# A two-layer cross-attention kernel on one core: TensorE's first loop holds one batch, its products become pairs, and one slot's order and one transpose move

## The chip, the cores and the metric

The kernel runs on one core of a Trainium2 chip. The metric is device microseconds of one execution. TensorE multiplies matrices into PSUM; VectorE (DVE), ScalarE (ACT) and GpSimd (POOL) do the elementwise work, and SyncE (SP) issues nearly all transfers. Each engine runs its own instruction stream in order and waits on counting semaphores.

## The reference

```python
x = x + _L0_xattn_ref(_layernorm(x), ctx_768, Wq, Wk, Wv, Wo, bo)     # 16 heads of 64, softmax over 77 keys
x = x + _L0_ffn_ref(_layernorm(x), w_gate, w_up, w_down)              # silu(gate) * up, hidden 768
x = x + _L1_xattn_ref(_layernorm(x), ctx_768, Wq, Wk, Wv, Wo, bo)
x = x + _L1_ffn_ref(_layernorm(x), rhs)                               # rounded to 8 bits, scaled back
```

x is 32 batches of 256 rows by 256 numbers (float32), the context 32 batches of 77 rows by 192. Layer 0 is the first two lines, layer 1 the last two.

## The kernel before

A first part (to about 210 us) computes the keys and values of both layers and prepares the weights. Every operand is split into a high and a low float16 part, so each product is three terms (high x high, high x low, low x high).

The main part walks through steps h = 0 to 65: steps 0 to 31 are the batches of layer 0, steps 32 to 63 those of layer 1. A step has four slots, u = 0 to 3, one for four heads each. Work on one batch is spread over several steps: in step h TensorE computes the scores of batch h, the queries of two slots ahead, the weighted values of three slots back, the output projection of batch h-1, and the feed-forward of batches h-2 and h-3. `lay[d]` is the layer of the batch at step h+d, or None. One step of layer 0 is called a batch below.

In the third slot (u = 2) of layer 0, TensorE's order is: scores of row tile 0, `down(0)` (the feed-forward's last product for rows 0 to 127; 12 products), the queries (12 products), scores of row tile 1, `down(1)` (12 products for rows 128 to 255), `gate_up(1)` (the feed-forward's first products for hidden columns 128 to 255; 8), `project` (12) and `weigh_values`. The names of the tiles: `kb` holds keys, `qT_h`, `qT_l` the queries' parts, `xT` the turned normalised rows that the queries are made from, `wdT` with `hT_h`, `hT_l` are the operands of `down`, `x2T` those of `gate_up`, `oT_h`, `oT_l` those of `project`, `pT` and `vb` those of `weigh_values`.

`product` writes a product either as one matmul of 128 columns of weights, or, with `halved`, as a pair of matmuls of 64 columns, each with its own half of PSUM's partitions. `weigh_values` is always pairs. In layer 0 the products of the third slot, `down` and `gate_up(1)` are whole, all others are pairs. (In the profile, L301 is a half of a pair, L299 a whole product, L1126 `down`.)

The results of `gate_up` and `down` go to two PSUM banks in turn. A program (`uses`, `released`) decides which: the order of uses in a step of layer 0 is gate_up(4), gate_up(5), gate_up(0), down(0), down(1), gate_up(1), gate_up(2), gate_up(3). A use waits until its bank's last use has been read. `down(1)` thus takes the bank of `gate_up(0)`, and waits on `s_hf`, which VectorE raises when `hidden(0)` (tile `hf`, L1320) has read that bank.

VectorE's order in the third slot: statistics of the next rows, `sigmoid_gate(0)`, `maxima` of row tile 0, `out_rows(0)` (reads `down(0)`'s bank, tile `y`, L1330), `shift` (`nmr`), the low part of `oT`, `hidden(0)` (`hf`), a reciprocal, `maxima` of row tile 1, the low part of the queries, `out_rows(1)`.

The turned rows `xT` have two buffers, used in turn by even and odd batches. SP issues the transposing transfer for batch h+2 in the last slot of step h (`turn_rows`), which waits on `s_q` until the buffer's last queries are made; the queries of batch h+1 in slot u = 2 wait on `s_xd` for theirs. SP also issues the transposes of the probabilities (`pT`), keys, values and rows, in one queue.

TensorE, ScalarE and VectorE run steps 4 to 27 and 36 to 59 as hardware loops whose body holds two steps (`bodies`, `LOOPS`); SP and GpSimd have all steps written out.

Of the kernel before, what the change touches and what calls it, by code (L numbers as in the profile page):

```python
# [40 lines left out]
P = 128  # L41
HEADS, DH = 16, 64
UNITS = 4
# [7 lines left out]
def xattn_ffn_kernel(nc, x, ctx, wq0, wk0, wv0, wo0, bo0, w_gate, w_up, w_down,  # L51
                     wq1, wk1, wv1, wo1, bo1, rhs, out):
    B, NQ, D = x.shape
# [27 lines left out]
    with stack:  # L81
# [184 lines left out]
        x_src = [x.rearrange("b (t p) d -> b p t d", p=P), mid_d.rearrange("b (t p) d -> b p t d", p=P)]  # L266
        def turned_rows(par, part):

            return xT[par][:, :, part, :, :]

# [9 lines left out]

        def turn_rows(sp, b):

            sp.wait_ge(s_x16l, b)
            after(sp, s_q, UNITS * (b - 1))
            sp.dma_start_transpose(xT[b % 2][:, :, :, :, :].rearrange("p t r k q -> p (t r k) q"),
                                   x16[:, :, :, :].rearrange("p t r d -> p (t r d)")).then_inc(s_xd, 16)
# [17 lines left out]
        def queries(pe, u, l, par, o, halved):  # L304
            for a in range(PPU):
                w = slice((u * PPU + a) * P, (u * PPU + a + 1) * P)
                oo = o[:, a, :].rearrange("p (t q) -> p t q", q=P)
                terms = [(ww, part, k) for k in range(KT) for ww, part in
                         ((wq_h[l], 0), (wq_h[l], 1), (wq_l[l], 0))]
                for q, (ww, part, k) in enumerate(terms):  # L310
                    last = product(pe, oo, ww[:, k, w], xT[par][:, :, part, k, :], halved, start=(q == 0),
                                   stop=(q == len(terms) - 1))
            last.then_inc(s_q, 1)
# [57 lines left out]
        with nc.Block() as block:  # L371
            @block.sync
            def _(sp):
# [57 lines left out]
                i = NG - 1  # L431
# [16 lines left out]
                load_rows(2)  # L448
                turn_rows(sp, 1)
                store_keys(i, 1, 1)  # L450
# [495 lines left out]
        for first, last in LOOPS:  # L946
            assert (last - first) % 2 == 0
            assert all(kinds[h] == kinds[first + (h - first) % 2] for h in range(first, last))

        def bodies(eng, body):  # L950

            done = 0
            for first, last in LOOPS:
                for h in range(done, first):
                    body(h, h, *kinds[h])
                with eng.Fori(first, last, 2) as h:
                    body(h, first, *kinds[first])
                    body(h + 1, first + 1, *kinds[first + 1])
                done = last
            for h in range(done, NB + 2):  # L960
                body(h, h, *kinds[h])

        with nc.Block() as block:

            @block.sync
            def _(sp):
# [33 lines left out]
                def body(h, like, lay, plan):  # L1000
# [13 lines left out]
                    for u in range(UNITS):  # L1014
# [14 lines left out]
                        if u == 0 and lay[-2] == 0:  # L1029
                            turn_second_rows(h - 2)  # L1030
                        if u == 1 and lay[0] is not None:
                            after(sp, s_pv, n - 2)
                            load_values(0, at_own, lay[0])
# [16 lines left out]
                        if u == 3 and lay[3] == 0:  # L1050
                            sp.wait_ge(s_xn, QT * (h + 3))
                            sp.dma_start(x_in[:, :, :], batch_of(x_src[0], b_first)).then_inc(s_x, 16)
                        if u == 3 and lay[2] == 0:
                            turn_rows(sp, h + 2)
                        if u == 2 and lay[-3] == 0:
# [11 lines left out]
            def _(pe):  # L1067
                def paired(u, lay):

                    return lay[0] == 1 or u != 2  # L1070

                def scores(k, u, t, k_need, halved):
# [13 lines left out]
                def project(k, u, l):  # L1086

                    pe.wait_ge(s_ol, k + 1)
                    for t in range(QT):
                        for a in range(PPU):  # L1090
                            ts, m = slice(t * P, (t + 1) * P), u * PPU + a
                            for q, (oo, ww) in enumerate(((oT_h[u % 2], wo_h[l]), (oT_l[u % 2], wo_h[l]),
                                                          (oT_h[u % 2], wo_l[l]))):
                                first = u == 0 and t == 0 and a == 0 and q == 0
                                last = product(pe, OA[:, t, :], oo[:, a, ts], ww[:, m, :], u != (1 if l == 1 else 2),
                                               start=first, stop=(u == UNITS - 1 and a == PPU - 1 and q == 2),
                                               skip_group_check=True)
                    if u == UNITS - 1:
                        last.then_inc(s_oa, 1)
# [14 lines left out]
                def gate_up(c, o):  # L1114
                    for a, w in ((0, wgT), (1, wuT)):
                        oo = o[:, a, :].rearrange("p (t q) -> p t q", q=P)
                        terms = [(k, part) for k in range(KT) for part in range(2)]
                        for q, (k, part) in enumerate(terms):
                            last = product(pe, oo, w[:, k, c * P:(c + 1) * P], x2T[:, :, part, k, :], c != 1,
                                           start=(q == 0), stop=(q == len(terms) - 1))  # L1120
                    last.then_inc(s_g, 1)

                def down(t, o):
                    terms = [(c, hh) for c in range(HC) for hh in (hT_h, hT_l)]
                    for q, (c, hh) in enumerate(terms):
                        last = pe.matmul(o[:, 0, :], hh[:, c, t * P:(t + 1) * P], wdT[:, c, :], start=(q == 0),  # L1126
                                         stop=(q == len(terms) - 1))
                    last.then_inc(s_d, 1)
# [8 lines left out]
                def body(h, like, lay, plan):  # L1137
                    n = UNITS * h

                    def bank(*use):  # L1140

                        where, before = plan[use]
                        if before is not None:
                            pe.wait_ge(*released(before[0], h + before[1]))
                        return RG[where]

                    for u in range(UNITS):
# [9 lines left out]
                        if u == 3 and lay[-2] == 0:  # L1157
                            gate_up(2, bank("gu", 2))
                        if ("q", u) in plan:
                            if u == 2 and lay[1] == 0:  # L1160
                                pe.wait_ge(s_xd, 16 * (h + 1))
                            if u == 2 and lay[1] == 1:
                                pe.wait_ge(s_xl, h + 3 - B)
                            queries(pe, (u + 2) % UNITS, lay[(u + 2) // UNITS], (like + (u + 2) // UNITS) % 2, bank("q", u), paired(u, lay))
                        if u == 2 and lay[-2] == 1:
# [29 lines left out]

                bodies(pe, body)


            @block.scalar
            def _(act):  # L1200
                def body(h, like, lay, plan):
# [27 lines left out]
                    for u in range(UNITS):  # L1229
# [28 lines left out]
                        if u == 1 and lay[1] == 1:  # L1258
                            act.wait_ge(s_xt, h + 3 - B)
                            high(act, turned_rows((like + 1) % 2, 0),  # L1260
                                 bank("turned_x", 0).rearrange("p k (t q) -> p t k q", q=P)).then_inc(s_xh, 1)
# [38 lines left out]
            def _(dve):  # L1300
                def body(h, like, lay, plan):
# [47 lines left out]
                    for u in range(UNITS):  # L1349
# [65 lines left out]
                        if u == 1 and lay[1] == 1:  # L1415
                            dve.wait_ge(s_xh, h + 3 - B)
                            low(dve, turned_rows((like + 1) % 2, 1),
                                bank("turned_x", 0).rearrange("p k (t q) -> p t k q", q=P),
                                turned_rows((like + 1) % 2, 0)).then_inc(s_xl, 1)
                        if u == 1 and lay[-1] == 1:  # L1420
# [131 lines left out]
```

## Time and profile before

| | |
|---|---|
| median of 3 runs | 1631.79 us (1630.43 to 1633.48) |
| the profiled execution | 1632.44 us, its span 1630.6 us |
| mean granted clock of TensorE | 0.994 of full speed |
| TensorE (PE) busy | 1568.4 us, 96% of the span |
| VectorE, ScalarE, GpSimd busy | 1358.4, 1379.6, 1270.9 us (83%, 85%, 78%) |
| TensorE's matmuls | 25178 |

A row of the timeline is one instruction, or several alike in a row: start in us from the span's beginning, time in us until the last of them ends, engine, line, operation, tiles, partitions by columns, count. Matmuls overlap: one takes 0.27 us from start to end, but the next starts 0.11 us after it, so what a product costs is the distance between starts. PE is the matmul, PEld the load of its weights, which runs ahead.

### The profile page before, as it was taken

The page shows a single profiled execution, that of the slowest core. Times are in us where ns is not written, and L with a number is a line of the kernel's source. Part 1 is how long each engine was busy: PE and PEld are TensorE (multiplying, and loading weights), DVE is VectorE, ACT ScalarE, POOL GpSimd, SP SyncE. Part 2 cuts the span into 40 slices and gives each one's busy share as a digit, 9 for nine tenths or more (in the row PEclk, how much of TensorE's full clock was granted, in tenths as well). Part 3 has the DMA queues.
Part 4 walks back from the last instruction along what each step waited for, and adds up shares of the span by engine and source line. Part 5 has one row for each costly group of instructions (what it writes and reads, how often), then busy time and mean ns, then how long its engine had stood idle before and what let it go on. Part 6 is the DMA issues. An engine that isn't in the chain of part 4 may idle for free.

```text
span 1630.6 us, 70351 instructions
## 1 busy us (share of the span) xinstructions
PE 1568.4 (96%) x25178; PEld 1420.3 (87%) x25178; DVE 1358.4 (83%) x3519; ACT 1379.6 (85%) x5665; POOL 1270.9 (78%) x1892
## 2 busy tenths in 40 slices
PE   7999978999999999999999999999999999999995
PEld 4655668999999999999999999989999999999994
DVE  5777767888888888888888887888899899989885
ACT  5665677889998998998898888888999999999993
POOL 3300058898998988988988988778999999999984
PEclk9999999999999999999999999999999999999998
DMA  8975679897787787787787988889899889989995
GB/s 239 324 281 226 223 183 170 169 176 174 172 175 178 165 179 176 166 180 172 166 181 171 176 168 160 151 173 193 190 200 199 190 190 200 199 189 190 197 182 107
DMA packets 732248, 305.79 MB, mean 188 GB/s; under 512 B 621424, under 2 KB 717584, under 8 KB 730064
## 3 DMA queue, kind: packets, MB, share of 16 engines
q1 hardware_dynamic: 730272, 297.29, 82.1%
q0 software_dynamic: 1840, 6.82, 1.3%
q8 instruction: 69, 1.13, 0.3%
q14 instruction: 67, 0.55, 0.1%
HBM read 87.72 MB, written 65.54 MB: 94 GB/s over the span
## 4 chain that ended last, share of the span: by engine, by line
PE 35%; POOL 30%; issue 12%; DVE 5%; DMA 3%; ACT 1%; POOLq 0%; SPq 0%; ACTq 0%; DVEq 0%
PE psum L301 24%; POOL pr L1481 10%; POOL p L1488 8%; POOL p L1484 6%; PE psum L1110 4%; PE psum L299 4%; POOL hT_l L1471 3%; POOL rs L361 2%; DMA pT<-p 2%; PE psum L1126 2%; PE psum L292 1%; DVE oT_l L330 1%; DVE x L1460 1%; POOL y L1509 1%; DMA x2T<-x 1%
## 5 line engine op out<-in xcount | busy, mean ns | idle before, releaser
L1225 ACT ACTIVATE ex<-psum,nmax 128x77 f32<-128x77 f32 x2048 | 638.0, 335 | 46.2 <-DVE nmax L1342 37.1
L1225 ACT ACTIVATION_READ_ACCUMULATOR ex<-psum,nmax 128x1 f32 x2048 | 443.1, 216 | 0.0
L1488 POOL TENSOR_TENSOR p<-pr,p 128x308 f16<-128x308 f32 x512 | 413.1, 807 | 38.4
L1481 POOL TENSOR_TENSOR pr<-ex,rden 128x308 f32<-128x308 f32 x512 | 369.1, 721 | 63.7 <-DVE rden L1347 63.1
L301 PE MATMUL psum<-xT,wq_h 128*64 128x256 f16 x3552 | 304.5, 273 | 0.0
L1342 DVE TENSOR_REDUCE nmax<-psum 128x4 f32<-128x308 f32 x512 | 241.2, 471 | 63.6 <-PE psum L301 53.7
L1484 POOL CAST p<-pr 128x308 f16<-128x308 f32 x512 | 241.7, 472 | 43.0 <-DMA pT<-p 10.7
L301 PE MATMUL psum<-xT,wq_l 128*64 128x256 f16 x1776 | 245.9, 273 | 0.0
L301 PE MATMUL psum<-kb,qT_h 128*64 128x154 f16 x3584 | 228.0, 231 | 11.1 <-DVE qT_l L333 6.9
L301 PE MATMUL psum<-wo_h,oT_h 128*64 128x256 f16 x1536 | 214.2, 275 | 12.2 <-DVE oT_l L330 11.2
L1110 PE MATMUL psum<-pT,vb 77*64 77x256 f16 x3072 | 213.0, 274 | 0.6 <-DMA pT<-p 0.6
L301 PE MATMUL psum<-wo_h,oT_l 128*64 128x256 f16 x1536 | 212.6, 273 | 0.0
L301 PE MATMUL psum<-wo_l,oT_h 128*64 128x256 f16 x1536 | 212.6, 273 | 0.0
L330 DVE TENSOR_TENSOR oT_l<-psum,oT_h 128x512 f16<-128x512 f32 x256 | 175.7, 686 | 24.8 <-ACT oT_h L316 24.1
L301 PE MATMUL psum<-kb,qT_l 128*64 128x154 f16 x1792 | 196.1, 230 | 0.0
L301 PEld LDWEIGHTS psum<-kb,qT_h 128*64 128x64 f16 x3584 | 179.8, 110 | 14.2 <-DVE qT_l L333 9.3
L301 PEld LDWEIGHTS psum<-xT,wq_h 128*64 128x64 f16 x3552 | 190.3, 110 | 0.8 <-issue 0.6
L316 ACT ACTIVATE oT_h<-psum 128x512 f16<-128x512 f32 x256 | 153.9, 601 | 26.1 <-PE psum L1110 19.5
L333 DVE SCALAR_TENSOR_TENSOR qT_l<-psum,qT_h 128x512 f16<-128x512 f32 x256 | 174.0, 680 | 0.0
L1110 PEld LDWEIGHTS psum<-pT,vb 77*64 77x64 f16 x3072 | 164.3, 110 | 11.0 <-issue 7.7
L316 ACT ACTIVATE qT_h<-psum 128x512 f16<-128x512 f32 x256 | 154.9, 605 | 1.0 <-PEq L371 1.0
L361 POOL TENSOR_TENSOR rs<-ve,half_neg 128x2 f32<-128x2 f32 x127 | 88.5, 696 | 56.4 <-DVE ve L346 52.9
(167 smaller groups left out, 3805.4 us busy)
## 6 DMA issues: line engine op xcount, KB each, us to landing
keys<-ks SPq DMA_DIRECT2D x16, 1232.0 KB, 5.3
kb<-keys SPq DMA_DIRECT2D x256, 77.0 KB, 2.6
vb<-vals SPq DMA_DIRECT2D x128, 154.0 KB
vals<-vs SPq DMA_DIRECT2D x64, 256.0 KB, 3.1
x_pair<-in_x_dram SPq DMA_DIRECT2D x32, 256.0 KB, 3.1
pT<-p SPq DMA_TRANSPOSE x512, 3.3
x_res<-in_x_dram SPq DMA_DIRECT2D x32, 256.0 KB, 3.0
mid_x<-y SPq DMA_DIRECT2D x32, 256.0 KB, 2.4
```

Source lines behind the costliest of these rows:

```text
L299: return pe.matmul(o, w, x, **flags)
L301: last = pe.matmul(o[b * DH:(b + 1) * DH], w[:, b * DH:(b + 1) * DH], x, **flags)
L316: return act.activation(dst, src, ACT.Copy, scale=scale)
L330: return dve.tensor_tensor(dst, src, hi, ALU.subtract)
L333: return dve.scalar_tensor_tensor(out=qT_l[i][:, :, :], in0=src, scalar=Q_DOWN, in1=qT_h[i][:, :, :], op0=ALU.mult, op1=ALU.subtract)
L361: pool.tensor_tensor(rs[:, :], ve[:, :], half_neg[:, :], ALU.pow).then_inc(s_inv[k], 1)
L1110: last = pe.matmul(OV[b * DH:(b + 1) * DH, a, :], vb[u // 2][:, part, c:c + DH], pT[u][0:NK, pp * HPU + hd, :], start=(q == 0), stop=(q == 2))
L1225: last = act.activation(ex[i][:, t, b, :], SC[:, t, b * NK:(b + 1) * NK], ACT.Exp, bias=nmax[i][:, t, b:b + 1], accum_out=den[i][:, t, b:b ...
L1342: dve.tensor_reduce(nmax[i][:, t, :], SC[:, t, :].rearrange("p (h k) -> p h k", k=NK), AX_X, ALU.max, negate=True).then_inc(s_m, 1)
L1481: pool.tensor_tensor(pr[:, t, :, :], ex[i][:, t, :, :], r, ALU.mult).then_inc(s_p, 1)
L1484: pool.tensor_copy(d[:, t, 0, :, 0:NK], pr[:, t, :, :]).then_inc(s_ph, 1)
L1488: pool.tensor_tensor(d[:, t, 1, :, 0:NK], pr[:, t, :, :], d[:, t, 0, :, 0:NK], ALU.subtract).then_inc(s_pl, 1)
```

## The change

- TensorE's loop over steps 4 to 27 has a body of one step (24 turns in place of 12). The other engines' loops, and TensorE's second loop, keep two steps.
- Every product of layer 0 in the loop, and `down` and `gate_up(1)`, is a pair of 64 columns.
- From batch 4 on, the turned rows have one buffer (`home`). Their transposing transfer is issued a step later than before, in SP's first slot behind the transpose of `x2T`, and waits on `s_q` until all queries of batch h (the last of them in TensorE's slot u = 1) are made.
- In the third slot of steps 3 to 33 (`late`), TensorE runs `down(1)` directly behind `down(0)`, and the queries behind the scores of row tile 1.

```diff
-        def turned_rows(par, part):
+        def home(b):
+            return 1 if b in (1, 3) else 0
+        def turned_rows(b, part):
-            return xT[par][:, :, part, :, :]
+            return xT[home(b)][:, :, part, :, :]
...
-        def turn_rows(sp, b):
+        def turn_rows(sp, b, like):
             sp.wait_ge(s_x16l, b)
-            after(sp, s_q, UNITS * (b - 1))
+            if like <= 4:
+                after(sp, s_q, UNITS * (like - 1))
+            else:
+                sp.wait_ge(s_q, UNITS * b)
...
-            for first, last in LOOPS:
+            for (first, last), step in zip(LOOPS, steps):
                 for h in range(done, first):
                     body(h, h, *kinds[h])
-                with eng.Fori(first, last, 2) as h:
-                    body(h, first, *kinds[first])
-                    body(h + 1, first + 1, *kinds[first + 1])
+                with eng.Fori(first, last, step) as h:
+                    for i in range(step):
+                        body(h + i if i else h, first, *kinds[first])
...
+                        if u == 0 and lay[1] == 0 and like >= 4:
+                            turn_rows(sp, h + 1, like + 1)
...
-                        if u == 3 and lay[2] == 0:
-                            turn_rows(sp, h + 2)
+                        if u == 3 and lay[2] == 0 and like <= 2:
+                            turn_rows(sp, h + 2, like + 2)
...
-                def paired(u, lay):
-                    return lay[0] == 1 or u != 2
...
-                                last = product(pe, OA[:, t, :], oo[:, a, ts], ww[:, m, :], u != (1 if l == 1 else 2),
+                                last = product(pe, OA[:, t, :], oo[:, a, ts], ww[:, m, :], l == 0 or u != 1,
...
-                            last = product(pe, oo, w[:, k, c * P:(c + 1) * P], x2T[:, :, part, k, :], c != 1,
+                            last = product(pe, oo, w[:, k, c * P:(c + 1) * P], x2T[:, :, part, k, :], True,
...
-                        last = pe.matmul(o[:, 0, :], hh[:, c, t * P:(t + 1) * P], wdT[:, c, :], start=(q == 0),
-                                         stop=(q == len(terms) - 1))
+                        last = product(pe, o[:, 0, :], hh[:, c, t * P:(t + 1) * P], wdT[:, c, :], True, start=(q == 0),
+                                       stop=(q == len(terms) - 1))
...
-                            scores(n + u, u, 0, 32 * (h + 1), paired(u, lay))
+                            scores(n + u, u, 0, 32 * (h + 1), True)
                         if u == 2 and lay[-3] == 0:
                             pe.wait_ge(s_hlp, len(LOW_POOL) * (h - 2))
                             pe.wait_ge(s_hld, len(LOW_DVE) * (h - 2))
                             down(0, bank("down", 0))
...
+                        late = u == 2 and lay[-3] == 0 and lay[-2] == 0
+                        if late:
+                            down(1, bank("down", 1))
+                        else:
+                            make_queries(u)
...
-                            scores(n + u, u, 1, 0, paired(u, lay))
+                            scores(n + u, u, 1, 0, True)
+                        if late:
+                            make_queries(u)
...
-                        if u == 2 and lay[-3] == 0:
+                        if u == 2 and lay[-3] == 0 and not late:
                             down(1, bank("down", 1))
...
-                bodies(pe, body)
+                bodies(pe, body, (1, 2))
```

TensorE's instructions in the third slot of a layer 0 step, before, from the end of the first scores on. In brackets stand the semaphores that an instruction waits for: `s_hf` for VectorE's `hf`, `s_xd` for the turned rows.

```order
L299 MATMUL psum<-kb,qT_l 128x154
...
L1126 MATMUL psum<-wdT,hT_h 128x256 [waits s_hf]
L1126 MATMUL psum<-wdT,hT_l 128x256
...
L299 MATMUL psum<-xT,wq_h 128x256 [waits s_ql,s_xd]
...
L299 MATMUL psum<-kb,qT_h 128x154 [waits s_e]
...
L1126 MATMUL psum<-wdT,hT_h 128x256 [waits s_hf]
L1126 MATMUL psum<-wdT,hT_l 128x256
```

The same place in the changed kernel:

```order
L308 MATMUL psum<-kb,qT_l 64x154 x2
...
L308 MATMUL psum<-wdT,hT_h 64x256 [waits s_hf]
L308 MATMUL psum<-wdT,hT_h 64x256
L308 MATMUL psum<-wdT,hT_l 64x256 x2
...
L308 MATMUL psum<-wdT,hT_h 64x256 [waits s_hf]
L308 MATMUL psum<-wdT,hT_h 64x256
L308 MATMUL psum<-wdT,hT_l 64x256 x2
...
L308 MATMUL psum<-kb,qT_h 64x154 [waits s_e]
...
L308 MATMUL psum<-xT,wq_h 64x256 [waits s_ql,s_xd]
```

The second `down`, with its wait on `s_hf`, stands ahead of the scores and the queries, which stood between the two `down`; whole products have become pairs.

VectorE's instructions around the same place, in the changed kernel (their order is that of before, and only the line numbers differ). `s_d` is TensorE's `down`, `s_oh` ScalarE's `oT_h`:

```order
L1356 TENSOR_REDUCE nmax<-psum 128x4 [waits s_s]
L1344 SCALAR_TENSOR_TENSOR y<-psum,y 128x256 [waits s_yx,s_d]
L358 SCALAR_TENSOR_TENSOR nmr<-mv,rs 128x2 [waits s_inv0]
L337 TENSOR_TENSOR oT_l<-psum,oT_h 128x512 [waits s_oh]
L1334 SCALAR_TENSOR_TENSOR hf<-psum,sg 128x256 [waits s_sg]
L1361 RECIPROCAL rden<-den 128x4 [waits s_e]
L1356 TENSOR_REDUCE nmax<-psum 128x4 [waits s_s]
```

Nothing moved here: `y` (which waits for `down(0)`) stands three instructions ahead of `hf` (for which `down(1)` waits).

SP's queue from one step's end into the next, before:

```order
L1052 DMA x_pair<-in_x_dram 128x2x256 [waits s_xn]
L285 DMA_TRANSPOSE xT<-x 128x8x128 [waits s_q,s_x16l]
L1020 DMA x_res<-in_x_dram 128x2x256 [waits s_x1]
L278 DMA kb<-keys 64x616 [waits s_s]
L278 DMA kb<-keys 64x616
L977 DMA_TRANSPOSE pT<-p_1 128x8x128 [waits s_pl,s_pv]
L985 DMA_TRANSPOSE x2T<-x 128x8x128 [waits s_g,s_x216l]
L977 DMA_TRANSPOSE pT<-p_1 128x8x128 [waits s_pl]
```

And in the changed kernel:

```order
L1061 DMA x_pair<-in_x_dram 128x2x256 [waits s_xn]
L1027 DMA x_res<-in_x_dram 128x2x256 [waits s_x1]
L282 DMA kb<-keys 64x616 [waits s_s]
L282 DMA kb<-keys 64x616
L984 DMA_TRANSPOSE pT<-p_1 128x8x128 [waits s_pl,s_pv]
L992 DMA_TRANSPOSE x2T<-x 128x8x128 [waits s_g,s_x216l]
L292 DMA_TRANSPOSE xT<-x 128x8x128 [waits s_q,s_x16l]
L984 DMA_TRANSPOSE pT<-p_1 128x8x128 [waits s_pl]
```

The transpose into `xT` moved five places down, behind that into `x2T`, and a transpose of probabilities now stands behind it.

## Rows read from the trace of the kernel before

**Rows 1.** Window of a batch: length; busy PE, PEld, DVE, ACT, POOL; clock; DMA.

```profile
497.10:521.90 24.80, 24.74 (x416) 23.30 (x412) 21.96 (x61) 22.36 (x94) 22.40 (x34) 1.00 0.78 173
```

**Rows 2.** Timeline of PE, third slot of one batch.

```profile
509.49 0.31 PE L299 MATMUL psum<-kb,qT_h 128*128 128x154 f16 x2
...
511.11 0.27 PE L1126 MATMUL psum<-wdT,hT_l 128*128 128x256 f16 x1
511.22 0.38 PE L299 MATMUL psum<-xT,wq_h 128*128 128x256 f16 x2
...
512.53 0.30 PE L299 MATMUL psum<-kb,qT_h 128*128 128x154 f16 x2
...
512.94 0.27 PE L1126 MATMUL psum<-wdT,hT_h 128*128 128x256 f16 x1
...
516.32 0.27 PE L299 MATMUL psum<-wo_l,oT_h 128*128 128x256 f16 x1
516.52 0.85 PE L1110 MATMUL psum<-pT,vb 77*64 77x256 f16 x12
```

**Rows 3.** Timeline of DVE, same slot.

```profile
511.42 0.42 DVE L1330 SCALAR_TENSOR_TENSOR y<-psum,y 128x256 f32<-128x256 f32 x1 [0.52 <-PE psum L1126]
511.76 0.16 DVE L351 SCALAR_TENSOR_TENSOR nmr<-mv,rs 128x2 f32<-128x2 f32 x1
511.84 0.68 DVE L330 TENSOR_TENSOR oT_l<-psum,oT_h 128x512 f16<-128x512 f32 x1
512.44 0.41 DVE L1320 SCALAR_TENSOR_TENSOR hf<-psum,sg 128x256 f32<-128x256 f32 x1
```

**Rows 4.** Timeline of PE, the next batch, from the end of down(0).

```profile
535.85 0.38 PE L299 MATMUL psum<-xT,wq_h 128*128 128x256 f16 x2
...
537.69 0.28 PE L1126 MATMUL psum<-wdT,hT_h 128*128 128x256 f16 x1
```

**Rows 5.** Waits of PEld, 300 to 900 us: in total, times, longest.

```profile
PEld psum L1110 <- issue: 5.1, 24, 0.2
PEld psum L301 <- DVE oT_l L330: 5.0, 24, 0.3
PEld psum L299 <- issue: 3.8, 19, 0.2
...
PEld psum L1126 <- DVE hf L1320: 1.7, 11, 0.2
PEld psum L299 <- ACT ex L1225: 1.0, 5, 0.2
```

**Rows 6.** Timeline of PE: queries as pairs, second slot.

```profile
504.44 0.38 PE L301 MATMUL psum<-xT,wq_h 128*64 128x256 f16 x4
...
505.74 0.30 PE L301 MATMUL psum<-kb,qT_h 128*64 128x154 f16 x4
```

**Rows 7.** Line 956 (the loops' branches) in 496.9 to 497.6 us: ns min/median/max, starts.

```profile
L956 PEldq COMPARE_BRANCH  x1: 215/215/215, 497.1 to 497.1; - x1
```

**Rows 8.** Timeline of PE around the branch at 497.10 us.

```profile
497.08 0.28 PE L301 MATMUL psum<-wo_l,oT_h 128*64 128x256 f16 x2
497.19 0.28 PE L301 MATMUL psum<-wo_h,oT_h 128*64 128x256 f16 x2
```

**Rows 9.** Timeline of PE, an idle stretch ahead of the loop.

```profile
254.96 0.47 PE L301 MATMUL psum<-kb,qT_h 128*64 128x154 f16 x4 [3.45 <-DVE qT_l L333]
```

**Rows 10.** Windows of PE there: us, busy, granted clock, DMA share, GB/s.

```profile
225.00:230.00 5.00, 3.28 (x66) 1.00 0.72 140
...
250.00:255.00 5.00, 1.55 (x30) 0.84 1.01 195
255.00:260.00 5.00, 5.00 (x58) 0.50 1.15 162
```

**Rows 11.** Timeline of SP, first two slots.

```profile
505.12 1.23 SPq L985 DMA_TRANSPOSE x2T<-x  x1
```

**Rows 12.** DMA issues: tiles, queue, kind, count, median us from issue to landing.

```profile
xT<-x SPq DMA_TRANSPOSE x31, 3.5
```

More of the change, by code:

```diff
@@ L279, in load_keys @@
                              keys_d[l][rows, b, g].rearrange("p r m k -> p (r m k)")).then_inc(s_kb[g], 16)
-        def turn_rows(sp, b):
+        def turn_rows(sp, b, like):
             sp.wait_ge(s_x16l, b)
-            after(sp, s_q, UNITS * (b - 1))
-            sp.dma_start_transpose(xT[b % 2][:, :, :, :, :].rearrange("p t r k q -> p (t r k) q"),
+            if like <= 4:
+                after(sp, s_q, UNITS * (like - 1))
+            else:
+                sp.wait_ge(s_q, UNITS * b)
+            sp.dma_start_transpose(xT[home(like)][:, :, :, :, :].rearrange("p t r k q -> p (t r k) q"),
                                    x16[:, :, :, :].rearrange("p t r d -> p (t r d)")).then_inc(s_xd, 16)
@@ L302, in product, with queries @@
             return last
-        def queries(pe, u, l, par, o, halved):
+        def queries(pe, u, l, b, o, halved):
             for a in range(PPU):
@@ L310, in queries @@
                 for q, (ww, part, k) in enumerate(terms):
-                    last = product(pe, oo, ww[:, k, w], xT[par][:, :, part, k, :], halved, start=(q == 0),
+                    last = product(pe, oo, ww[:, k, w], xT[home(b)][:, :, part, k, :], halved, start=(q == 0),
                                    stop=(q == len(terms) - 1))
@@ L448, in _ @@
                 load_rows(2)
-                turn_rows(sp, 1)
+                turn_rows(sp, 1, 1)
                 store_keys(i, 1, 1)
@@ L947, in xattn_ffn_kernel, with bodies @@
             assert (last - first) % 2 == 0
-            assert all(kinds[h] == kinds[first + (h - first) % 2] for h in range(first, last))
-        def bodies(eng, body):
+            assert all(kinds[h] == kinds[first] for h in range(first, last))
+        def bodies(eng, body, steps=(2, 2)):
             done = 0
-            for first, last in LOOPS:
+            for (first, last), step in zip(LOOPS, steps):
                 for h in range(done, first):
                     body(h, h, *kinds[h])
-                with eng.Fori(first, last, 2) as h:
-                    body(h, first, *kinds[first])
-                    body(h + 1, first + 1, *kinds[first + 1])
+                with eng.Fori(first, last, step) as h:
+                    for i in range(step):
+                        body(h + i if i else h, first, *kinds[first])
                 done = last
@@ L1145, in bank, with make_queries @@
                         return RG[where]
+                    def make_queries(u):
+                        if ("q", u) in plan:
+                            if u == 2 and lay[1] == 0:
+                                pe.wait_ge(s_xd, 16 * (h + 1))
+                            if u == 2 and lay[1] == 1:
+                                pe.wait_ge(s_xl, h + 3 - B)
+                            queries(pe, (u + 2) % UNITS, lay[(u + 2) // UNITS], like + (u + 2) // UNITS, bank("q", u), True)
                     for u in range(UNITS):
@@ L1158, in body @@
                             gate_up(2, bank("gu", 2))
[L1159 to L1164, printed above, removed]
+                        late = u == 2 and lay[-3] == 0 and lay[-2] == 0
[3 more added lines that the diff above has]
+                            make_queries(u)
                         if u == 2 and lay[-2] == 1:
@@ L1259, in body @@
                             act.wait_ge(s_xt, h + 3 - B)
-                            high(act, turned_rows((like + 1) % 2, 0),
+                            high(act, turned_rows(like + 1, 0),
                                  bank("turned_x", 0).rearrange("p k (t q) -> p t k q", q=P)).then_inc(s_xh, 1)
@@ L1416, in body @@
                             dve.wait_ge(s_xh, h + 3 - B)
-                            low(dve, turned_rows((like + 1) % 2, 1),
+                            low(dve, turned_rows(like + 1, 1),
                                 bank("turned_x", 0).rearrange("p k (t q) -> p t k q", q=P),
-                                turned_rows((like + 1) % 2, 0)).then_inc(s_xl, 1)
+                                turned_rows(like + 1, 0)).then_inc(s_xl, 1)
                         if u == 1 and lay[-1] == 1:
```

## The prediction

> **What bounds the kernel now.** I read first the windows, to see which engine has no idle time; then TensorE's timeline through the one slot whose order changes; then VectorE's through the same slot, because `down(1)` waits for it; then the waits and the transfers.
>
> In a batch of layer 0 TensorE is busy for 24.74 of 24.80 us, while VectorE, ScalarE and GpSimd have 2.4 to 2.8 us to spare [rows 1]. So TensorE sets the pace of steps 4 to 27 and nearly so of those around them: time that it loses there is time of the kernel, and so is time that it is given, until one of the other three takes over.
>
> In the third slot the last product of `down(0)` starts at 511.11 and the queries at 511.22, the scores of row tile 1 at 512.53, `down(1)` at 512.94 [rows 2]. So 1.31 us of queries and 0.41 us of scores, 1.72 together, lie between the two `down`.
>
> VectorE meanwhile starts `out_rows(0)` (tile `y`) at 511.42: it had stood idle for 0.52 us, waiting for `down(0)`. Behind it come `nmr`, `oT_l`, and at 512.44 `hidden(0)` (tile `hf`), which ends at 512.85 [rows 3]. This is what `down(1)` waits for, as its bank is that of `gate_up(0)`. The reader is to see that `hf` cannot be ready before `down(0)` is done, since VectorE works in order and `y` stands ahead of it. In the batch shown `down(1)` comes 0.09 us after it. In the next batch it even waits for it: `down(0)` ends at 535.85 and `down(1)` starts at 537.69, 1.84 later instead of 1.72 [rows 4], and the list of waits has 11 of 24 batches in which `down`'s weights waited for `hf` [rows 5]. So the queries and scores between the two `down` cover a delay of just their own length.
>
> **The change, part by part.**
>
> *`down(1)` directly behind `down(0)`.* Nothing that `down(1)` waits for comes earlier: `y` still waits for `down(0)`, and takes 0.34 us to the next start, `nmr` 0.08, `oT_l` 0.60, `hf` 0.41 [rows 3]. With the 0.20 from the product's end to `y` and about 0.06 from `hf`'s end to the matmul (0.09 is the bound from the first batch) that is 1.69 us; the second batch measured 1.84 [rows 4]. TensorE, which works in order, stands idle for that long. `down(1)` starts as late after `down(0)` as it did before, and the 1.72 us of scores and queries, which used to fill the gap, come behind it. Queued behind the wait are these scores (VectorE's maxima, then ScalarE's exponentials wait for them), the queries, `gate_up(1)`, `project` and `weigh_values`; all of them move back together. The cost is 1.72 us for each batch, less 0.03 where `down(1)` had not waited before. It has `late` in steps 3 to 33, 31 of them: 31 x 1.72 = 53.3, less 13 x 0.03 = 0.4, +52.9 us. Its cover is gone altogether: no other instruction of TensorE stands between.
>
> *Whole products become pairs.* A product costs the same either way: 12 query products as pairs take 505.74 - 504.44 = 1.30 us [rows 6], 12 whole ones 512.53 - 511.22 = 1.31 [rows 2]. What goes is the passage from one form to the other. Out of the whole form: 0.20 us from 516.32 to 516.52 where a product takes 0.11 [rows 2], so 0.09, and this comes in all 24 batches (5.1 us of idle weight loads, 0.21 each) [rows 5]. Into it, at the first scores: also about 0.2 of idle, 24 times (19 put down to issue, 5 to ScalarE) [rows 5], so 0.1. With 0.02 to 0.03 that the first product behind each passage is slow (the four-product rows above don't resolve it; I take 0.02), 0.21 a batch. For 32 batches 6.7 us, and in steps 32 to 34, where `down` and `gate_up(1)` alternate with pairs, up to four passages each at 0.1, 1 more: -7.7 us. A rule on the same thing stands in the Trainium skill, TensorEngine Tiling (Array Packing), Key Properties: a change of tiling mode drains TensorE. The trace agrees in direction, and gives the size that the page leaves out. By that rule alone the change would be a gain, which is the first rival below.
>
> *One step per turn of the loop.* The branch at 497.1 takes TensorE's queue 0.22 us [rows 7], but its matmuls go on every 0.11 us through it [rows 8], because the queue is ahead of the matmuls. Twelve more branches stand at the same place of a step (behind `project`'s issue), with the same work queued: 0. If that cover were gone, 12 x 0.22 = 2.6 us. The idle time at `down(1)` does not take it, as it lies two slots away.
>
> *One buffer for turned rows, and a later transpose.* SP issues it once it has issued `x2T`'s (505.12, taking 1.23, so at 506.35) [rows 11] and the queries of slot two are done, which is at 505.74 plus their tail [rows 6]. It lands 3.5 us later [rows 12], at about 509.9. The queries wanted it at 511.22 before [rows 2], and now want it 1.7 + 1.3 + 0.4 later, at 514.6. So no wait, 4.7 us to spare. The transposes of probabilities behind it move back by 1.23 us; the earliest of these is wanted by `weigh_values` at 516.5 [rows 2], and has landed by about 511. Cost 0; bound above, if GpSimd is held by a late buffer and this reaches TensorE, 0.3 us a batch (a quarter of the 1.23).
>
> *The others.* VectorE had waited 0.52 us for `down(0)` in this slot [rows 3], so it and ScalarE come to it with no backlog, and start from the same place. Behind `down(1)` all move back by the same 1.6 us, so no new wait follows. The small wait for `oT_l` in slot two (0.2 a batch, 24 times, of which 0.1 is the normal step) [rows 5] may go if the others are further ahead: between 0 and -3 us.
>
> **Sum.** 52.9 - 7.7 = +45.2 us, and I take 1 off for the last steps, where the chain to `hf` may be as short as 1.61 (0.20 + 0.34 + 0.60 + 0.41 + 0.06, with `nmr` gone). The profiled execution took 1632.4 us (its span 1630.6), which gives 1676.6; against the median of 1631.8, 0.6 lower, 1676.
>
> **Rivals.**
>
> *The wait is not what binds, only the passages count (not slower).* Then -7.7 us, 1624. It would take `hf` ready when `down(0)` ends, at 511.22, and it decides for this side once the gap left uncovered is under 0.25 us a batch. For it speaks only that the tiling rule names a gain. Against: `hf` ends at 512.85, 1.63 late, behind an instruction that itself needs `down(0)` [rows 3]. 2 in 100.
>
> *The others catch up in the idle time.* The chain falls to 1.61 in each batch, and the waits for `oT_l` go: -3 - 3, with some at `x2T`, 1668. `nmr` took 0.08 here [rows 3] and was worth more in the other batch. 1 in 10.
>
> *A second wait joins.* A late buffer for the probabilities, or VectorE short of time in the fourth slot: 0.3 us x 31 = 9, 1685. Against: 1.6 us more a batch for engines that had 2.4 to 2.8 spare [rows 1]. 1 in 10.
>
> *TensorE's clock falls in the new gaps.* Ahead of the loop it fell to 0.50 (1.2 GHz in place of 2.4) after 3.45 us of idle [rows 9, 10], and stayed there for the window of 5 us and about 1.6 before. That would cost half of 6.6 us, 31 times: +102, 1778. Against: a window with 1.72 us of idle kept 1.00 [rows 10]. 2 in 100.
>
> *The branches show.* Each of 12 more waits for code: as long as a transfer at most (3.5 us [rows 12] for want of a nearer row), +42, 1718. The Trainium skill, Runtime: NRT & Kernel Launch, Instruction fetch mechanics, says that a taken branch whose target lies outside the fetched window stalls. The trace shows no such stall at the branches that there are [rows 8], and the body is now shorter. 2 in 100.
>
> **How the numbers follow.** My forecast has 74 in 100, with its own range 1671 to 1682. The two neighbours have 10 each, the others 6 in all. The range 1665 to 1688 takes in both neighbours. A measurement of this kernel tells about 0.2%, 3 us, from no change; only the first rival is faster (0.02), 0.01 for chance agreements, so slower 0.97.
>
> **What the changed profile would show.** In the third slot, `y` 0.2 us behind `down(0)`, and PE idle for 1.6 to 1.8 us ahead of the second `down`, released by `hf` (as a wait, some 50 us in 31 times); the batch at 26.3 in place of 24.8 us; no idle weight load of 0.2 at the slot's two ends; 27354 matmuls (68 more in each of 32 batches); clock 1.00 throughout; no wait for `xT`; layer 1 as before. I would be wrong if the idle time ahead of `down(1)` is short, if a wait for `oT_l` or `x2T` grows by more than 0.3 us, or if the clock row shows a fall.

## The result and the profile after

The changed kernel takes 1678.2 us (median of 4 runs, 1677.8 to 1680.0), the kernel before 1631.4 beside it: ratio 1.0293, with a 95% interval of 1.0277 to 1.0308. Forecast were 1676 us, in a range of 1665 to 1688. The profiled execution took 1678.4 us, its span 1676.6.

The windows, one batch of the loop (from one second `down` to the next) and one of layer 1; the columns are length, busy time of PE, PEld, DVE, ACT and POOL, granted clock, DMA share and GB/s:

```profile
501.90:528.30 26.40, 24.72 (x480) 24.05 (x480) 21.35 (x61) 22.24 (x93) 22.48 (x34) 1.00 0.73 159
...
1200.60:1218.70 18.10, 17.94 (x346) 17.39 (x342) 16.25 (x42) 16.86 (x79) 16.54 (x26) 1.00 0.88 196
```

Against 24.74 of 24.80 us [rows 1], TensorE is busy for as long as it was, 24.72 us, but the batch takes 26.40: what was added is time in which TensorE stands idle. The clock is at 1.00. TensorE's timeline in the third slot has the stretch:

```profile
526.40 0.28 PE L308 MATMUL psum<-wdT,hT_l 128*64 128x256 f16 x2
528.33 0.30 PE L308 MATMUL psum<-wdT,hT_h 128*64 128x256 f16 x2 [1.65 <-DVE hf L1334]
...
529.67 0.30 PE L308 MATMUL psum<-kb,qT_h 128*64 128x154 f16 x4
...
530.08 0.38 PE L308 MATMUL psum<-xT,wq_h 128*64 128x256 f16 x4
```

The last product of `down(0)` starts at 526.40, so it is done at 526.51, and the first of `down(1)` starts at 528.33, 1.82 us later. (The 1.65 of the row counts from the matmul's modelled end.) VectorE's timeline at the same place:

```profile
526.72 0.42 DVE L1344 SCALAR_TENSOR_TENSOR y<-psum,y 128x256 f32<-128x256 f32 x1 [0.41 <-PE psum L308]
527.06 0.28 DVE L358 SCALAR_TENSOR_TENSOR nmr<-mv,rs 128x2 f32<-128x2 f32 x1
527.27 0.68 DVE L337 TENSOR_TENSOR oT_l<-psum,oT_h 128x512 f16<-128x512 f32 x1
527.87 0.41 DVE L1334 SCALAR_TENSOR_TENSOR hf<-psum,sg 128x256 f32<-128x256 f32 x1
528.20 0.16 DVE L1361 RECIPROCAL rden<-den 128x4 f32<-128x4 f32 x1
530.28 0.48 DVE L1356 TENSOR_REDUCE nmax<-psum 128x4 f32<-128x308 f32 x1 [1.92 <-PE psum L308]
```

It is the chain of [rows 3], in the same order: `y` behind `down(0)`, `nmr`, `oT_l`, `hf`. Only `nmr` is longer, 0.28 in place of 0.16. (From batch to batch `nmr` is short and long by turns: in the next batch it is 0.41 us here, and was 0.31 before.) New is that VectorE now stands idle in its turn, 1.92 us, for the scores of row tile 1, which TensorE makes behind `down(1)`: two engines wait for each other by turns. The waits over the whole execution (total, times, longest):

```profile
PEld psum L308 <- DVE hf L1334: 60.6, 31, 2.8
PE psum L308 <- DVE hf L1334: 52.3, 31, 2.5
```

31 times, as many as there are steps with `late`. The starts of the matmuls on both sides of the stretch, less the 0.11 us that a product takes, give 57.3 us of lost time, 1.85 each: in the loop 1.68 to 1.83 and 1.94 to 1.95 by turns, 1.68 and 1.61 in the last steps, and once, in step 3 ahead of the loop (at 289 us), 2.68. In the list for 300 to 900 us the idle weight loads of [rows 5] look like this:

```profile
PEld psum L308 <- DVE hf L1334: 45.4, 23, 2.1
...
PEld psum L308 <- DVE oT_l L337: 5.1, 23, 0.4
PEld psum L308 <- issue: 3.9, 12, 1.5
```

The 24 stretches of 0.21 ahead of `weigh_values` (L1110 before) are gone, and those ahead of the first scores too; the wait for `oT_l` is what it was. TensorE's waits for `x2T` over the whole execution, before and after, did change:

```profile
PE psum L301 <- DMA x2T<-x: 1.2, 4, 0.5
PE psum L308 <- DMA x2T<-x: 3.2, 3, 1.2
```

The three of the changed kernel come at 260.8, 283.8 and 312.4 us, ahead of the loop and in its first turn, and none comes behind them. This is 2.0 us more, in one execution of each kernel. The prediction had named growth of this wait by more than 0.3 us as a sign of being wrong, and the sign is there, though small. The transfers, and the loop's branch in 300 to 950 us:

```profile
520.54 1.23 SPq L992 DMA_TRANSPOSE x2T<-x  x1
521.87 1.31 SPq L292 DMA_TRANSPOSE xT<-x  x1
523.23 2.71 SPq L984 DMA_TRANSPOSE pT<-p  x2
```

```profile
L963 PEldq COMPARE_BRANCH  x24: 83/215/242, 327.3 to 935.4; - x24
```

The transpose of the turned rows stands where it was forecast; with 3.3 us to landing it is there at 525.2, 4.9 us ahead of the queries at 530.08, and nothing waits for it. The branches take the queue what they took [rows 7]. From the first to the last branch are 23 batches: (935.4 - 327.3) / 23 = 26.44 us a batch. In the same way the kernel before has 24.82, (894.1 - 348.1) / 22. This length of a batch is given for the experiments below. It comes from one profiled execution of each kernel, so its noise was not measured; kernels that should be equal (before and e6, e4 and e8) agree to 0.01 us. The whole execution tells some 3 us.

### The profile page after: what moved, and what is told of

Its sections match the earlier page's. It is cut to its first block, busy times and chain, and to the rows that moved or that the text cites. A ratio compares the mean times of both kernels' runs of the same rounds, so it can differ in the third digit from the quotient of the medians.

```text
span 1676.6 us, 74775 instructions
## 1 busy us (share of the span) xinstructions
PE 1563.3 (93%) x27354; PEld 1444.9 (86%) x27354; DVE 1340.0 (80%) x3519; ACT 1381.0 (82%) x5665; POOL 1275.0 (76%) x1892
## 4 chain that ended last, share of the span: by engine, by line
PE 60%; DVE 8%; issue 7%; POOL 6%; ACT 4%; DMA 2%; SPq 1%; ACTq 0%; POOLq 0%; DVEq 0%
PE psum L308 49%; PE psum L1115 7%; DVE oT_l L337 3%; PE psum L306 2%; POOL pr L1495 2%; ACT ex L1239 1%; PE psum L299 1%; POOL p L1502 1%; POOL p L1498 1%; DVE nmr L358 1%; DVE x L1474 1%; DMA pT<-p 1%; ACT yn L327 1%; POOL rs L368 1%; DMA x2T<-x 1%
## 5 line engine op out<-in xcount | busy, mean ns | idle before, releaser
L308 PE MATMUL psum<-xT,wq_h 128*64 128x256 f16 x4064 | 347.3, 272 | 0.0
L308 PE MATMUL psum<-xT,wq_l 128*64 128x256 f16 x2032 | 281.2, 273 | 0.0
L308 PE MATMUL psum<-kb,qT_h 128*64 128x154 f16 x4096 | 260.3, 231 | 12.5 <-DVE qT_l L340 4.9
L308 PE MATMUL psum<-wo_h,oT_h 128*64 128x256 f16 x1792 | 250.4, 275 | 13.2 <-DVE oT_l L337 12.4
L308 PE MATMUL psum<-wo_l,oT_h 128*64 128x256 f16 x1792 | 249.1, 274 | 0.0
L308 PE MATMUL psum<-wo_h,oT_l 128*64 128x256 f16 x1792 | 249.0, 274 | 0.0
L308 PE MATMUL psum<-kb,qT_l 128*64 128x154 f16 x2048 | 224.1, 229 | 0.0
L308 PEld LDWEIGHTS psum<-kb,qT_h 128*64 128x64 f16 x4096 | 205.7, 109 | 15.7 <-DVE qT_l L340 8.0
L308 PEld LDWEIGHTS psum<-xT,wq_h 128*64 128x64 f16 x4064 | 217.4, 110 | 0.0
L337 DVE TENSOR_TENSOR oT_l<-psum,oT_h 128x512 f16<-128x512 f32 x256 | 175.7, 686 | 26.3 <-ACT oT_h L323 24.8
L323 ACT ACTIVATE oT_h<-psum 128x512 f16<-128x512 f32 x256 | 154.1, 602 | 23.3 <-PE psum L1115 13.5
L368 POOL TENSOR_TENSOR rs<-ve,half_neg 128x2 f32<-128x2 f32 x127 | 97.8, 770 | 65.6 <-DVE ve L353 62.5
```

The lines of the kernel that those rows point to most:

```text
L323: return act.activation(dst, src, ACT.Copy, scale=scale)
L337: return dve.tensor_tensor(dst, src, hi, ALU.subtract)
L368: pool.tensor_tensor(rs[:, :], ve[:, :], half_neg[:, :], ALU.pow).then_inc(s_inv[k], 1)
```

## The experiments

| kernel | median us | ratio to before (95%) | batch, us |
|---|---|---|---|
| changed kernel | 1678.2 | 1.0293 (1.0277 to 1.0308) | 26.44 |
| e1: the old order, rest changed | 1627.3 | 0.9974 (0.9963 to 0.9986) | 24.70 |
| e2: the new order alone | 1684.2 | 1.0317 (1.0299 to 1.0335) | 26.52 |
| e3: pairs alone, two-step loop | 1670.5 | 1.0238 (1.0223 to 1.0253) | 26.67 |
| e4: changed, hidden(0) early | 1623.3 | 0.9943 (0.9930 to 0.9956) | 24.55 |
| e5: scores between the two down | 1664.3 | 1.0210 (1.0190 to 1.0230) | 26.02 |
| e6: one-step loop and one buffer alone | 1628.8 | 0.9992 (0.9982 to 1.0002) | 24.82 |
| e7: as e1, two-step loop | 1678.8 | 1.0302 (1.0285 to 1.0319) | 27.19 |
| e8: as e1, hidden(0) early | 1622.0 | 0.9953 (0.9940 to 0.9967) | 24.56 |
| e9: as e3, down whole | 1690.7 | 1.0374 (1.0346 to 1.0401) | 27.50 |
| e10: as e9, queries, project whole | 1713.2 | 1.0505 (1.0487 to 1.0522) | 28.26 |

### e1: the old order back

```diff
-                        late = u == 2 and lay[-3] == 0 and lay[-2] == 0
+                        late = False
```

> The changed kernel with the third slot's order of before: the queries and the second scores again between the two down. Theory (the wait for hf costs the 1.72 us that stood between them; the pairs alone save 0.21 us a batch): no idle stretch of more than 0.15 us ahead of the second down, ratio to the kernel before about 0.9953 (1624 us). Rival A (the single buffer, the later transpose or the one-step loop cost something too, hidden so far in the idle time): a wait for xT at the queries or idle time at the loop's end, ratio 0.998 to 1.01. Rival B (the passages between whole products and pairs are not what costs the 0.2 us at the slot's ends): ratio 1.000.

It is faster than before, so the order alone had turned the sign. But it is 0.26% and not 0.47%, and the idle time ahead of the second `down` is not under 0.15 us. TensorE's timeline of it, in one batch, and PEld's in the next:

```profile
511.29 0.24 PE L308 MATMUL psum<-kb,qT_l 128*64 128x154 f16 x2
511.44 0.30 PE L308 MATMUL psum<-wdT,hT_h 128*64 128x256 f16 x2
```

```profile
536.09 0.11 PEld L308 LDWEIGHTS psum<-wdT,hT_h 128*64 128x64 f16 x2 [0.25 <-DVE hf L1334]
```

In the second, `hf` comes 1.88 us behind the end of `down(0)`, where it had come at 1.78 before; in the first 1.74 in place of 1.63. VectorE's timeline there shows `nmr` at 0.41 us, where the kernel before has 0.31 in the same batch:

```profile
536.39 0.31 DVE L351 SCALAR_TENSOR_TENSOR nmr<-mv,rs 128x2 f32<-128x2 f32 x1
```

The rows of e1:

```profile
534.35 0.42 DVE L1344 SCALAR_TENSOR_TENSOR y<-psum,y 128x256 f32<-128x256 f32 x1 [0.41 <-PE psum L308]
534.69 0.41 DVE L358 SCALAR_TENSOR_TENSOR nmr<-mv,rs 128x2 f32<-128x2 f32 x1
535.03 0.68 DVE L337 TENSOR_TENSOR oT_l<-psum,oT_h 128x512 f16<-128x512 f32 x1
```

and the waits in 300 to 900 us have `nmr` waiting for GpSimd's `rs` (its reciprocal root), 1.4 us in 9 times in the kernel before, 6.0 in 23 here:

```profile
DVE nmr L358 <- POOL rs L368: 6.0, 23, 0.3
```

My reading: the slot begins 0.1 us earlier, `down(0)` is done 0.1 earlier, but `rs` is not, and the chain to `hf` is as much longer. So nearly half of the 0.21 us that the passages should have given is given back at the second `down`. Of rival A there is no sign: no wait for `xT`. e6 and e8 measure the two apart.

### e2: the new order alone

```diff
+                        if late:
+                            down(1, bank("down", 1))
+                        else:
+                            make_queries(u)
...
                             scores(n + u, u, 1, 0, paired(u, lay))
+                        if late:
+                            make_queries(u)
```

> The kernel before with only the new order of the third slot: whole products in that slot, two buffers, two-step loop stay. Theory: PE idle for 1.7 to 1.85 us ahead of the second down in 31 steps, +53 us, 1684 us, ratio 1.032. Rival (part of the loss is due to the later transpose in the transfer queue or to the one-step loop): under 1.028.

1684.2 us. The whole loss is in the order, and a little more than the loss of the change; the passages between whole products and pairs are still there. Its waits in 300 to 900 us:

```profile
PEld psum L1126 <- DVE hf L1329: 43.3, 23, 2.0
```

### e5: how much cover each piece gives

```diff
                             scores(n + u, u, 1, 0, True)
                         if late:
+                            down(1, bank("down", 1))
                             make_queries(u)
```

> The changed kernel with the scores of row tile 1 put back between the two down, and the queries left behind them. Theory (the stretch is what the chain over VectorE takes, about 1.86 us, less what lies between the two down): the 0.42 us of scores shorten the idle stretch to 1.44 us, 31 x 0.42 = 13 us less than the changed kernel, 1665 us, ratio to before 1.020. Rival (moving the queries behind the scores is the loss, whatever lies between the down): no gain, ratio 1.029.

1664.3 us, 13.9 less than the changed kernel's median (by the ratios 1.0293 and 1.0210, 13.5), and 0.42 us a batch, which is the 0.41 us that the scores take [rows 2]. Its waits, beside the 45.4 of the changed kernel:

```profile
PEld psum L308 <- DVE hf L1333: 34.5, 23, 1.6
```

### e4: hf made early

```diff
                         if u == 2 and lay[-2] == 0:
                             sigmoid_gate(0, h - 2)
+                            hidden(0, h - 2)
...
-                        if u == 2 and lay[-2] == 0:
-                            hidden(0, h - 2)
```

> The changed kernel with its new order, but VectorE makes hidden(0) directly behind sigmoid_gate(0), ahead of the maxima and of out_rows(0). Theory (down(1) waits only because hf stands behind an instruction that needs down(0)): hf is ready about 1 us ahead of down(0)'s end, the idle stretch ahead of the second down is gone, and the time falls by about 52 us to 1625, ratio 0.996. Rival (something else holds down(1), or hidden(0) in its new place delays the maxima and so the exponentials by as much): the stretch stays at 0.5 us or more a step, ratio over 1.01.

1623.3 us, 0.9943. TensorE's order is that of the change, word for word, and the loss is gone, with some 9 us more (0.57% of 1632). It was the place of one instruction on VectorE, behind one that needs `down(0)`, that made the new order dear. In 300 to 900 us one wait for `hf` of 0.5 us is left.

### e6: the loop and the buffer alone

The diff is the change without its pairs and without `late`.

> The kernel before with only the one-step loop, the one buffer for turned rows and its later transpose; whole products in the third slot and the old order. Theory (these three are hidden): ratio 1.000 within 0.002. Rival A (the second transpose in SP's queue or the twelve more branches cost some 0.1 us a batch, which would explain why pairs in the old order gave 4 to 6 us in place of 8): ratio 1.002 to 1.004.

0.9992, interval 0.9982 to 1.0002, 24.82 us a batch as before. The one-step loop, the one buffer and the transpose's new place cost nothing that these runs can tell. (TensorE does wait 1.9 us in 2 times for `x2T` in its trace, ahead of the loop, against 1.2 in 4 before.) From e6 to e1 only the pairs are added: 24.82 to 24.70, 0.12 us a batch, 0.18% or 3 us in all.

### e8: the old order, hf made early

e1 with e4's edit of VectorE's order.

> All pairs, one-step loop, the old order of TensorE, and VectorE makes hidden(0) directly behind sigmoid_gate(0). Theory (what the old order still lost, 0.1 to 0.25 us ahead of the second down in each batch, was hf coming late): no wait there, the same as the new order with hidden(0) early, batch of 24.55 us, ratio 0.9943. Rival (TensorE's new order is itself worth something once the wait is gone): slower than that one by over 0.1%.

24.56 us a batch, 0.26 less than e6, and the same as e4. The second `down` follows the scores without a gap, and VectorE's `hf` lies ahead of `y`:

```profile
608.92 0.31 PE L308 MATMUL psum<-kb,qT_h 128*64 128x154 f16 x4
609.05 0.24 PE L308 MATMUL psum<-kb,qT_l 128*64 128x154 f16 x2
609.12 0.28 PE L308 MATMUL psum<-wdT,hT_h 128*64 128x256 f16 x2
```

```profile
606.39 0.42 DVE L1323 SCALAR_TENSOR_TENSOR sg<-th,psum 128x256 f32<-128x256 f32 x1
606.84 0.42 DVE L1334 SCALAR_TENSOR_TENSOR hf<-psum,sg 128x256 f32<-128x256 f32 x1
607.19 0.47 DVE L1356 TENSOR_REDUCE nmax<-psum 128x4 f32<-128x308 f32 x1
607.61 0.42 DVE L1344 SCALAR_TENSOR_TENSOR y<-psum,y 128x256 f32<-128x256 f32 x1
```

With `hf` out of the way, TensorE's order makes no difference that can be told: 0.9953 and 0.9943, with intervals that overlap, and batches 0.01 us apart. Both are faster than the two kernels compared.

### e3: the pairs alone, in the loop of two steps

```diff
-                    return lay[0] == 1 or u != 2
+                    return True
```

and pairs for `down`, `gate_up(1)` and `project`.

> The kernel before with all products of layer 0 as pairs, in the two-step loop, two buffers, old order. Theory (pairs save the passages, whatever the loop): 27354 matmuls, ratio about 0.9953, the same as the kernel with the one-step loop and the old order within 0.1%. Rival (a two-step body of pairs only is too long for TensorE's code fetch, so that the one-step loop is needed): idle time of PE at or behind the branch in each turn, ratio over 0.997, or slower than before.

My theory fell: 1670.5 us, 38 us slower than before. The rival's sign is there. The branches, in 300 to 950 us, and the queue of TensorE's code (69 packets before, 71 in the changed kernel):

```profile
L956 PEldq COMPARE_BRANCH  x12: 83/3630/4282, 347.5 to 934.2; - x12
```

```profile
q8 instruction: 185, 3.03, 0.8%
```

The branch back takes 3.63 us (median) in place of 0.22 [rows 7], and the matmuls that are queued run out. (The 83 ns are the last branch, which leaves the loop; 11 go back.) TensorE's timeline behind the branch at 506.7 and the windows around it:

```profile
507.10 0.83 PE L1110 MATMUL psum<-pT,vb 77*64 77x256 f16 x12
510.37 1.07 PE L301 MATMUL psum<-x2T,wgT 128*64 128x256 f16 x8 [2.44 <-issue]
511.22 1.07 PE L301 MATMUL psum<-x2T,wuT 128*64 128x256 f16 x8
```

```profile
500.00:505.00 5.00, 5.00 (x106) 5.00 (x102) 4.40 (x13) 4.50 (x16) 4.62 (x7) 1.00 0.70 142
505.00:510.00 5.00, 2.93 (x56) 2.66 (x50) 3.99 (x10) 3.49 (x14) 4.04 (x7) 1.00 0.96 177
510.00:515.00 5.00, 4.63 (x64) 4.29 (x66) 1.77 (x7) 2.17 (x10) 1.06 (x3) 0.66 1.17 204
```

Behind the stretch of 2.44 us the clock is at 0.66 of full speed in the mean, the lower level for part of the window, and the four products of L301 take 0.85 us (511.22 - 510.37), twice what they took. A rule of the Trainium skill (Runtime: NRT & Kernel Launch, Instruction fetch mechanics) says that a taken branch whose target is not in the fetched window stalls until it is fetched; this trace agrees, with more code packets and 3.6 us a branch.

Of the 11 branches, 7 are followed by such a window of 0.66, behind idle stretches of 2.44 to 3.21 us, and 4 are not, behind stretches of 2.41 to 2.76 us:

```profile
404.00:409.00 5.00, 4.80 (x68) 4.54 (x70) 2.13 (x7) 2.21 (x10) 1.45 (x3) 0.66 1.03 200
617.00:622.00 5.00, 3.81 (x75) 3.59 (x77) 3.11 (x10) 3.08 (x12) 2.26 (x4) 1.00 0.94 212
```

So the loss has two parts: TensorE stands idle for 33.2 us in 15 stretches put down to issue (350 to 940 us), and the lower clock costs some 12 us, an estimate from the windows: 7 x 5.00 x (1 - 0.66).

### e7, e9, e10: is it the length of the body?

e7 is e1 with `bodies(pe, body, (2, 2))`.

> All pairs, the old order, one buffer and the later transpose, but TensorE's first loop of two steps. Theory (the branch of a body with 1996 recorded instructions takes 3.6 us, the buffers have no part in it): branches of 3 to 4 us, ratio 1.022 to 1.025, as with two buffers. Rival (the two-step pairs lost time by the order of the transposes): ratio 0.997 to 0.999.

The one buffer and the later transpose do not help: branches of 3.89 us, 185 packets, 1.0302. It is slower than e3 by more than was expected, 0.52 us a batch. The longer branches do not explain it: the idle time put down to issue is the same (33.6 us in 350 to 940 us, 33.2 in e3). What the two traces differ in is waits of TensorE for `x2T`, 4.3 us where e3 has none (0.2 a batch), and for `oT_l`, 2.0 us (0.1), and the lower clock, which lasts for 37 us of the loop in place of 24; at half speed this is an estimated 7 us lost, 0.3 a batch. Together that is no less than the 0.52. So in a loop of two steps the one buffer and the later transpose may cost something; which of them does was not separated.

e9 is e3 with `down` whole, as it was before; e10 has queries and `project` whole too. The numbers of instructions are those recorded on TensorE between two branches, matmuls, weight loads and its sequencer's own: 1724 in the kernel before (of which 824 are matmuls), 1001 in the changed one, 1996 in e3, 1900 in e9, 1804 in e10.

> The kernel before, two-step loop, two buffers, old order; all products of layer 0 pairs except down, so that the loop's body has 1900 recorded TensorE instructions (1724 before, 1996 with all pairs). Theory (the branch back is slow from some length of the body on, and this is past it): branches of 3 to 4 us, 185 code packets, ratio 1.02 or more. Rival (the limit lies close under 1996, or it is the pairs of down that hurt in a two-step loop): branches of 0.2 us, about 70 packets, ratio about 1.00, a few more passages between pairs and whole products.

> As the one with down whole, but queries and project whole too: scores and gate_up(1) are the only new pairs, and the body has 1804 recorded instructions. Theory: the branch is fast or slow by the length alone; if 1900 is slow and 1804 is fast, the limit lies between them. If both are slow, it lies between 1724 and 1804. Where the branch is fast the ratio is within 1.000 and 1.008 (two to four more passages of 0.1 us a step).

Both are slow, with medians of 4.03 and 4.10 us a branch and 172 and 170 code packets:

```profile
L956 PEldq COMPARE_BRANCH  x11: 3915/4101/4410, 350.5 to 915.8; - x11
```

So the branch is fast with 1724 recorded instructions in the body and slow with 1804, and it is not a matter of `down`'s form. Nor is it that of pairs as such: the changed kernel's body is all pairs and fast. The length of the body is what is left, though no run lengthened a body by anything but pairs. Both are slower than e3 although their bodies are shorter. Part of it is that each passage between whole products and pairs costs 0.09 to 0.10 us, and e9 has four a step, e10 six, against none: 0.4 and 0.6 us a batch of the 0.8 and 1.6. The traces show two more parts: TensorE's waits for `x2T`, 3.7 and 10.3 us in 350 to 940 us where e3 has none, 0.2 and 0.5 a batch, and more time at the lower clock.

## Why the prediction was right, point by point

*The mechanism.* `down(1)` waits for `hf`, which stands behind `out_rows(0)` on VectorE, and this is the loss: shown by e2 (the order alone loses it), e1 (the rest does not), e5 (the 0.41 us put between takes 0.42 off) and e4 (moving `hf` alone takes all of it off).

*Its size.* The step had 1.69 to 1.84 us idle and 1.72 of lost cover, 52.9 us in all. Measured are 1.85 idle and 1.73 a batch (26.44 against 24.70 of e1), 50.9 us between the two medians, which were taken on different occasions (52 by their ratios to the kernel before); e2, with whole products, has 1.70 a batch (26.52 against 24.82) and 52 us. The idle stretch was 0.1 us longer than I worked out, because the chain runs through `nmr`, which waits longer for GpSimd's `rs` in the kernels of pairs (in e2 the stretches in the loop are 1.68 to 1.84 us). This cancels against the same wait in e1, so that the cost of the order was right to 2 us.

*Passages between whole products and pairs.* Worked out were 0.21 us a batch, -7.7 us. This is the term that was mis-sized: the pairs gave 0.12 us a batch and 3 us (e6 to e1), since I took the time that they free for time of the kernel. In this slot TensorE did not set the pace alone: `hf` was already late in 11 of 24 batches [rows 5], and what is gained ahead of it is waited out behind. With `hf` early too the gain is 0.26 (e6 to e8). I put 0.2 of it down to the passages and the rest to the wait that the kernel before already had (1.84 against 1.72 us in every other batch, 0.06 in the mean); this division is an estimate, as no run has `hf` early with whole products. In the changed kernel the pairs gave 0.08 a batch and some 4 us (e2 to the changed kernel, by the ratios; 6 by the medians) where I had 7.7. This is about what separates 1676 from 1678, within the 3 us that a comparison can tell.

*One step per turn, one buffer, the later transpose.* Costed at nothing, and nothing that can be told was measured (e6: 0.9992, interval 0.9982 to 1.0002), beside the small waits for `x2T` ahead of the loop. But the loop's part had a reason that I did not see: I asked what twelve more branches cost, and not what the longer body would cost if they were not there. All pairs in the two-step loop lose 38 us (e3). The rival that had the branches show was priced for the wrong kernel; here it stayed at zero, as the row of L963 says.

*The others.* The clock stayed at 1.00 in the new gaps (also in 285 to 295 us, around the one of 2.68). The rival of the clock was priced by a row that I read too favourably: the clock was already down 1.6 us before the end of that stretch of 3.45 [rows 9, 10], so less than 3.45 us of idle had been enough, and e3 shows it. The wait for `oT_l` is 5.1 us against 5.0, and layer 1 is the same. The batch was 26.44 where 26.3 was expected. That the total came within 2 us is closer than a term wrong by 4 us allows one to expect, and is in part luck; the direction, the path and the cost of the order are not.

## What to carry to other kernels

Before moving an instruction ahead on one engine, follow its wait to the releasing engine and look at what stands ahead of the release there: if that needs the instruction which it is moved next to, all that lay between was cover, and is lost. Time taken off ahead of a wait is worth something only once the wait is gone; the two edits belong together, and the cheap one may be on the other engine. Before making a loop's body longer, look at how long its branch takes: here it jumped, from 0.22 us to 3.6 and more, and did not grow with the length.

## What the runs showed of the hardware

- TensorE's branch back to the loop's head takes 0.22 us with 1001 or 1724 recorded instructions in the body, and 3.6 to 4.1 us (medians) with 1804 to 1996; TensorE's code packets go from about 70 to 170 to 185. Where the limit lies between 1724 and 1804 was not measured.
- In e3, idle stretches of 2.44 to 3.21 us behind 7 branches were followed by the lower clock (0.66 in the mean of the next 5 us), and those of 2.41 to 2.76 us behind 4 others were not, so the length of the stretch alone did not decide. The stretches of 1.7 to 2.0 us in the changed kernel's loop, 26 us apart, and its one of 2.68 us left the clock at 1.00. What decides was not separated.
- A passage between products of 128 columns and pairs of 64 costs 0.09 to 0.10 us either way: in the kernel before the starts are 0.20 us apart from `gate_up` to the whole scores and from whole `project` to `weigh_values`, where a product takes 0.11.
